# Gated feed-forward over 16 tiles: x tiles 2 and 3 turned by DMA, the first two tiles in units of one, all engine orders laid out anew

## The reference

```python
s[b,n,m] = sigmoid(ctx[b,n]·Wi + ctx[b,m]·Wj + b)          # 512 x 512 for each batch
x = x + tanh(g_xattn) * (0.6 * s + 0.4 * layernorm(x))
z = layernorm(x)
# bitlinear(z, w): z is RMS-normalised and rounded to 8 bit by its row's maximum,
#                  w is rounded to -1, 0, 1 by the mean of |w|; then z @ w.T
gate = silu(bitlinear(z, w1));  up = bitlinear(z, w2)        # 512 -> 1408
x = x + tanh(g_ffn) * bitlinear(gate * up, w3)               # 1408 -> 512
```

## Time and profile before

| | us |
|---|---|
| median of 3 runs | 162.61 (161.21 to 162.77) |
| the profiled execution | 162.48 |
| its span (first to last instruction) | 160.7 |
| PE busy | 140.9 (88%) |
| DVE / ACT / POOL busy | 118.8 / 109.6 / 101.6 |

### The profile page before, as it was taken

The page is one execution under the profiler, slowest core; times in us unless marked ns, Lnnn a source line. Parts: engine busy times, 40 slices in busy tenths (PEclk is TensorE's granted clock), DMA queues, the critical chain, the costliest instruction groups (busy, mean ns, idle before and its releaser), DMA issues.

```text
span 160.7 us, 2420 instructions
## 1 busy us (share of the span) xinstructions
PE 140.9 (88%) x751; PEld 75.6 (47%) x751; DVE 118.8 (74%) x166; ACT 109.6 (68%) x179; POOL 101.6 (63%) x148
## 2 busy tenths in 40 slices
PE   0914877697889999999999999999999999999991
PEld 0813646356455544445444444445444444444540
DVE  0027899999968999897688997979966646509441
ACT  3178989799963999581997969887656536537320
POOL 3000993899997899968736996596899535450300
PEclk9999999879999999999999999999999999999999
DMA  4999999996179264591460827535259460426323
GB/s 132 319 398 394 409 401 418 374 384 237 31 138 142 56 122 86 112 150 64 90 155 7 213 81 193 109 70 150 57 110 152 90 155 2 82 72 160 117 79 131
DMA packets 44149, 26.67 MB, mean 166 GB/s; under 512 B 34663, under 2 KB 36712, under 8 KB 44136
## 3 DMA queue, kind: packets, MB, share of 16 engines
q1 hardware_dynamic: 44128, 26.52, 60.0%
q10 hardware_dynamic: 8, 0.00, 0.0%
HBM read 13.89 MB, written 4.19 MB: 113 GB/s over the span
## 4 chain that ended last, share of the span: by engine, by line
PE 70%; POOL 12%; DMA 7%; DVE 6%; issue 2%; SPq 1%; DVEq 0%; POOLq 0%
PE ps L1220 44%; PE ps L1254 24%; DMA raw_room<-in_L_ffn_w_dram 7%; POOL raw L493 4%; DVE w_abs L933 3%; POOL w3q L496 2%; DVE bn L890 1%; POOL xq L478 1%; DVE c_all L914 1%; POOL ln_r L424 1%; POOL c_all L439 1%; SPq L283 1%; POOL rnorm L448 1%; POOL slope L427 1%; PE ps L1162 0%
## 5 line engine op out<-in xcount | busy, mean ns | idle before, releaser
L1220 PE MATMUL ps<-w1T,xqT 128*128 128x512 f16 (+1 forms) x192 | 42.3, 372 | 0.0
L1220 PE MATMUL ps<-w2T,xqT 128*128 128x512 f16 (+1 forms) x192 | 40.6, 361 | 0.0
L984 DVE SCALAR_TENSOR_TENSOR raw<-ps,deq,raw_room 128x1408 f32<-128x1408 f32 x16 | 26.9, 1684 | 18.5 <-PE ps L1220 13.2
L1254 PE MATMUL ps<-w3T,hqT 128*128 128x512 f16 x176 | 39.9, 379 | 0.0
L505 POOL TENSOR_SCALAR hq<-raw,h_scale 128x1408 f16<-128x1408 f32 x15 | 23.6, 1576 | 13.6 <-DVE h_scale L994 13.2
L702 ACT ACTIVATE junk<-raw 128x1410 f16<-128x1410 f32 x16 | 22.0, 1376 | 13.7 <-DVE raw L984 13.7
L1220 PEld LDWEIGHTS ps<-w1T,xqT 128*128 128x128 f16 x192 | 19.1, 101 | 20.7 <-issue 2.2
L691 ACT ACTIVATE raw_room<-ps,deq 128x1408 f32<-128x1408 f32 x16 | 22.8, 1428 | 8.6 <-PE ps L1220 8.6
L1220 PEld LDWEIGHTS ps<-w2T,xqT 128*128 128x128 f16 x192 | 18.7, 98 | 19.5
L1254 PEld LDWEIGHTS ps<-w3T,hqT 128*128 128x128 f16 x176 | 17.1, 98 | 19.4 <-issue 0.2
L991 DVE TENSOR_REDUCE h_top<-raw 128x1 f32<-128x1409 f32 x16 | 25.8, 1612 | 0.2
(11 more groups left out here) (97 smaller groups left out, 180.9 us busy)
## 6 DMA issues: line engine op xcount, KB each, us to landing
c_all<-in_x_dram SPq DMA_DIRECT2D x16, 256.0 KB, 9.4
out_dram<-out_ring SPq DMA_DIRECT2D x16, 256.0 KB, 2.4
raw<-in_L_ffn_w_dram SPq DMA_DIRECT2D x4, 704.0 KB, 11.2
raw_room<-in_L_ffn_w_dram SPq DMA_DIRECT2D x3, 768.0 KB, 8.4
raw<-in_L_ffn_w_dram SPq DMA_DIRECT2D x3, 768.0 KB, 11.1
hq<-in_ctx_dram SPq DMA_DIRECT2D x4, 256.0 KB, 9.7
raw_room<-in_L_ffn_w_dram SPq DMA_DIRECT2D x1, 512.0 KB, 10.5
raw<-in_L_ffn_w_dram SPq DMA_DIRECT2D x1, 512.0 KB, 10.6
```

What stands on the lines that cost most here:

```text
L984: v.scalar_tensor_tensor(out=hid[:, t % HS, 0:H], in0=ps_up[:, 0:H], scalar=deq[:, 1, t:t + 1], in1=gate[:, t % GATES, :], op0=ALU.mult, o ...
L1220: last = m.matmul(bank[:, lo:hi], xqT[:, i % XT, k, :], wT[w][:, k, lo:hi], start=(k == 0), stop=(k == KD - 1))
L1254: last = m.matmul(ps_y[t % 2], hqT[:, t % HT, k, :], w3T[:, :, k, :], start=(k == 0), stop=(k == KH - 1))
```

## The change

Tiles 2 and 3 are turned by DMA (BY_PE 4 to 2). Tiles 0 and 1 are units of their own. affine_x moves: POOL has ten tiles (0 to 5, 8, 9, 14, 15) in place of eight, ACT four (6, 7, 10, 11) in place of eight, DVE two (12, 13). The splits of the weights' sums, conversions and evacuations are changed; POOL converts all four rows of w3. Every engine's list is written anew: on PE last_product(0) stands behind gate_product(6), and up_product(0) comes ahead of gate_product(1). add_x is done by DVE for eight tiles in place of six and by POOL for six in place of eight. The loads are as they were.

```diff
-    UNITS = [(0, 2), (2, 4), (4, 6), (6, 8), (8, 10), (10, 12), (12, 14), (14, 16)]
+    UNITS = [(0, 1), (1, 2), (2, 4), (4, 6), (6, 8), (8, 10), (10, 12), (12, 14), (14, 16)]
-    BY_PE = 4
+    BY_PE = 2
-    SGROUPS = [(0, 2), (2, 4), (4, 8), (8, 12), (12, 16)]
+    SGROUPS = [(0, 1), (1, 2), (2, 4), (4, 8), (8, 12), (12, 16)]
-    AFFINE_ACT = [4, 5, 6, 7]
-    AFFINE_DVE = []
+    AFFINE_ACT = [4, 6]
+    AFFINE_DVE = [7]
-    ABS_ACT = [[(0, 0, 3), (1, 3, 5), (2, 6, 8), (3, 10, 11)], [(0, 0, 3), (3, 9, 11)], [(0, 0, 1), (1, 1, 2)]]
-    ABS_DVE = [[(1, 5, 6), (2, 8, 9), (3, 9, 10)], [(1, 3, 6), (2, 6, 9)], [(2, 2, 3), (3, 3, 4)]]
+    ABS_ACT = [[(0, 0, 3), (1, 5, 6), (2, 8, 9), (3, 10, 11)], [(0, 0, 3), (1, 3, 6), (3, 9, 11)], [(0, 0, 1), (2, 2, 3), (3, 3, 4)]]
+    ABS_DVE = [[(1, 3, 5), (2, 6, 8), (3, 9, 10)], [(2, 6, 9)], [(1, 1, 2)]]
-    CONV_DVE = [[0, 3, 5], [2, 3], [0, 3]]
-    CONV_POOL = [[1, 2, 4], [0, 1, 4, 5], [1, 2]]
-    OUT_DVE = [[3, 5], [2]]
-    OUT_ACT = [[0, 1, 2, 4], [0, 1, 3, 4, 5]]
+    CONV_DVE = [[0, 2, 4], [0, 5], []]
+    CONV_POOL = [[1, 3, 5], [1, 2, 3, 4], [0, 1, 2, 3]]
+    OUT_DVE = [[0, 2, 4], [0, 5]]
+    OUT_ACT = [[1, 3, 5], [1, 2, 3, 4]]
```

More of the change, by code:

```diff
@@ L567, in _ @@
-            add_x(0)
-            quant_h(2)
-            add_x(1)
-            dequant_x(3)
-            mean_x(2)
-            slopes_x(3)
+            step_x(2)
+            dequant_x(2)
+            quant_h(0)
+            conv_w(2, 1)
+            quant_x(4)
+            conv_w(2, 2)
+            mean_x(0)
+            quant_x(5)
+            mean_x(1)
+            step_x(3)
+            dequant_x(3)
+            conv_w(2, 3)
+            slopes_x(4)
+            quant_x(6)
+            step_x(4)
@@ L1054, in _ @@
             weight_factor(1)
-            conv_w(2, 0)
-            weight_factor(2)
-            half_scores(2)
-            evac_w(1, 2)
-            clip_w3(0)
-            max_x(1)
-            stats_x(3)
-            clip_w3(1)
-            conv_w(2, 3)
-            clip_w3(2)
-            intercept(2)
-            clip_w3(3)
-            hidden(0)
-            half_scores(3)
-            max_h(0)
-            intercept(3)
-            make_x(2)
-            hidden(1)
-            max_x(2)
@@ L1074, in _ @@
-            max_h(1)
-            make_x(3)
-            hidden(2)
-            max_x(3)
+            make_x(2)
+            half_scores(2)
+            max_x(2)
+            hidden(0)
+            stats_x(5)
+            intercept(3)
+            max_h(0)
+            hidden(1)
+            make_x(3)
+            clip_w3(0)
+            max_x(3)
+            hidden(2)
+            intercept(4)
+            clip_w3(1)
+            half_scores(3)
+            stats_x(6)
+            hidden(3)
+            make_x(4)
@@ L1078, in _ @@
+            clip_w3(2)
+            max_x(4)
+            hidden(4)
+            clip_w3(3)
+            max_h(1)
+            weight_factor(2)
+            intercept(5)
             max_h(2)
-            stats_x(4)
-            hidden(3)
-            stats_x(5)
+            hidden(5)
             max_h(3)
-            stats_x(6)
-            hidden(4)
-            stats_x(7)
-            intercept(4)
-            max_h(4)
-            intercept(5)
-            hidden(5)
-            make_x(4)
@@ L1101, in _ @@
+            stats_x(8)
+            max_h(7)
+            max_x(6)
+            hidden(8)
+            add_x(2)
             intercept(7)
-            max_h(7)
-            hidden(8)
+            affine_x(12)
             max_h(8)
-            make_x(6)
-            max_x(6)
+            affine_x(13)
             hidden(9)
+            intercept(8)
             make_x(7)
@@ L1110, in _ @@
             max_x(7)
+            add_x(6)
             hidden(10)
```

430 lines of the change are left out of this document (217 added, 213 removed).

## The result

The changed kernel takes 160.91 us (median of 4, 160.05 to 161.08) against 162.69 (161.21 to 162.95) for the kernel before on the same chip: ratio 0.9895 [0.9847, 0.9943]. It is faster by about 1%, where 3.2% (157.4 us) was forecast, and its median lies at the very end of the stated range of 155.4 to 160.9. The profiled execution took 161.08 us, with a span of 159.3.

The account below looks back on a forecast made before the run. PE was taken as the bound from up_product(0) on, starting at U = 38.0 us; adding 114.3 of fixed PE work, 3.3 after the last product and 1.8 outside the span (119.4) gave 157.4 us, range 155.4 to 160.9.

Parts of the forecast that it names:

- PE bounds, and time = U + 119.4: From up_product(0) on PE never waits; fixed PE work 114.3, after the last product 3.3, outside the span 1.8 us.
- U: Start of up_product(0), which needs all of w2 transposed and copied; forecast 38.0 us, ends 36 and 40.7.
- Step 1: DVE at the start: w1's scale ready at 15.9 us, some 0.4 earlier, as stats_x(0) moves into idle time.
- Step 2: DVE from w1's scale to w2's: 10.2 us of work plus 2.0 of delays beside POOL, ready at about 28.1.
- Step 3: POOL from w1's scale through slopes_x(2) (to 28.4) to its last w2 conversion, conv_w(1,4), ending at 35.8 us.
- Step 4: PE and ACT ahead of up 0: ACT's evacuations end at 37.7 to 38.1, PE's work at 37.8; U = 38.0.
- So none of these becomes a wait.: Behind U, the checked work of DVE, POOL, ACT and DMA turns arrives in time; smallest margins 1.8 and 2.1 us.
- The margins: Slack behind U: gate 6 ends at 71; tile 2 has 1.8, w3's last row 2.1, the tail 0.7 us.
- If it were fast, nothing would change: Gate 0 left at 4.2 us at PE's lower clock; its length is covered, as PE waits for quant_x(1) afterwards.
- (b): Shared port holds DVE and POOL back in the weights' part, or a thin margin breaks: 160.1 us, chance 0.17.
- (c): w2's chain no faster; only PE's visible 1.24 wait and 0.8 of turn_x go: 160.8 to 162, chance 0.08.
- (d): Slower: DVE and POOL block each other where PE takes a tile in 4.75 us: 164 us, chance 0.05.

Follow-up runs that it names:

- e12: Changed kernel with store(1) ahead of turn_h(5) in SP's list and stats_x(5) behind hidden(1) on DVE: 159.35 us, ratio 0.9828 to the kernel before.
- e13: e12's kernel plus one-tensor-input intercepts, gate product 0 computed twice, clip_w3(3) ahead of hidden(4), turn_w3(3) ahead of turn_x(6): 158.88 us, ratio 0.9755 to the kernel before.
- e8: Changed kernel with one-tensor-input intercepts and gate product 0 computed twice around turn_w(1,0): 159.32 us, ratio 0.9841 to the kernel before.
- e3: Changed kernel with tiles 2 and 3 turned by PE and copied by ACT again (BY_PE 4): 162.91 us, ratio 1.0036 to the kernel before.
- e1: Changed kernel with one move in SP's list, store(1) ahead of turn_h(5): 158.77 us, ratio 0.9771 to the kernel before.
- e9: Changed kernel with store(1) ahead of turn_h(5), stats_x(5) behind hidden(1), one-tensor-input intercepts and gate product 0 twice: 159.81 us, ratio 0.9817 to the kernel before.
- e11: Changed kernel with gate product 0 computed twice and nothing else: 162.36 us, ratio 0.9943 to the kernel before.
- e2: Changed kernel with intercept as one tensor_scalar per tile (one tensor input) instead of one two-tensor instruction: 161.99 us, ratio 0.9856 to the kernel before.

## Why the prediction was off, step by step

- *PE bounds, and time = U + 119.4.* Right in form: in the profiled execution the 47 products and the small work went without a gap except at the two places. With the two waits taken out, e12 gives 39.39 + 119.4 = 158.8 for 159.29 measured, e13 36.97 + 119.4 = 156.4 for 157.20. The sum is 0.5 to 0.8 short, spread over small PE work.
- *Step 1, w1's scale at 15.9.* Right (16.04) for this execution. That it varies from 14.65 (e8) to 16.56 (e3) over the profiled kernels, by the landing of one load, I hadn't seen and gave no width.
- *Step 2, w2's scale at 28.1.* The mechanism was right, a term was mis-sized: 2.0 us of delays from shared work of DVE and POOL. I counted one intercept (0.7), two conversions (0.8) and one make_x (0.5). DVE's conversions weren't slowed (0.80, and 1.52 for two) and make_x took 0.75. But there were two intercepts in such places, 1.31 and 1.24, each 1.0 above the 0.26 that it takes with one tensor input, and two waits for POOL, 0.56 and 0.75. That is 3.3 in place of 2.0; cheaper evacuations and small instructions give some 0.4 back. With w1's scale 0.1 late this makes the 1.0 us.
- *Step 3, POOL's last w2 conversion at 35.8.* Same cause, in the other direction: slopes_x(2) was booked at 1.9 us (26.5 to 28.4) and took 3.1 (28.09 to 31.20), of which 1.69 is one 128x2 instruction that met DVE's make_x and pair of conversions. It began 1.6 late, behind step 2's delay. The 1.0 booked for the conversions beside them wasn't needed: they took 2.78 and 2.79, undisturbed. 37.6 in place of 35.8.
- *Step 4, U = 38.0.* It followed from step 3: 39.54. ACT ends its w2 evacuations at 39.5 too, so both roads were late together.
- *"So none of these becomes a wait."* This is the step that failed, and it cost 1.8 us, as much as U did. I had checked DVE, POOL, tiles 2 and 3, w3's last row and the tail, and none of these became a wait in the changed kernel: last 0 and last 14 begin without one. I had not checked the stretch from 71 to 110, where the last products run beside gate and up, and in it the loop SP (turn_h ahead of store), ACT (finish ahead of silu), POOL (dequant_h ahead of quant_h). e1 shows it: after one exchange in SP's list the wait of 1.4 is gone, and the median is 2.1 lower. The 0.4 ahead of up 2 is the same kind of miss on DVE: hidden(1) stood behind stats_x(5), intercept(3) and max_h(0), and with stats_x(5) moved (e12) the wait is gone.
- *The margins.* The end of gate 6 was forecast as U + 13 x 2.377 + 2.0 = 71, and it came at 70.6, but that is luck. From up 0 to gate 6 there are 12 products, not 13, so the sum should have read U + 30.5 = 68.5; U's 1.5 and the 0.4 ahead of up 2 made up the difference. By the forecast's own numbers w3's last row, landing at 68.9, would have been 0.4 late where a margin of 2.1 was given, and the margin for hidden(5) was 1.4, not 3.9. In the changed kernel the transpose was issued at 66.16 and landed 3.6 later, 0.8 ahead of last 0 (70.59). Where it took 5.3 to land, PE waited 0.54 to 1.23 (e3, e8, e9, e11).
- *PE's clock.* "If it were fast, nothing would change" was wrong in an instructive way. In the changed kernel gate 0 took 3.54 (forecast 4.2), and PE idled 2.20 afterwards. But in e2's profiled execution, where it took 2.54, the idle gap grew to 3.23, the clock fell, and what was won on the intercept was lost.
- *Rivals.* (b), port and thin margins at 160.1, comes closest in its causes: the shared work of DVE and POOL, and a wait behind U, though not one of those whose margins I had worked out. It is 0.8 short in the time (160.91), and I gave it 0.17. (The chances of the rivals under 161.0 add up to 0.90; I wrote 0.88.) (c), that only the DMA turning and the visible wait go (160.8 to 162, 0.08), has the right time but the wrong reason: the head did gain. At 41.93, behind up 0, PE had 46 products left, as many as the kernel before had at 45.64: 3.7 us earlier. Of that 1.8 was given back as the two waits, and the rest of the difference to the 1.4 us between the two profiled executions is small PE work. (d) didn't happen: PE was busy 30.77 of 31.00 in 40 to 71.

## What to carry to other kernels

In an engine's ordered list, and above all in the DMA queue's, ask of each entry what stands right ahead of it and whether *that* is ready: a store that frees a buffer belongs ahead of a transpose whose input is still being made. When all waits up to some point have been checked, check the rest of the span in the same way; the first unexamined stretch is where the gain goes. A small instruction with two tensor inputs next to GpSimd's large ones costs as much as a large one, and making it cheap pays only if what stands behind it doesn't meet the same instruction. And an engine that gets ahead of what feeds it can lose more by its clock than it won: read the granted clock of every trace before an edit is judged.
